# Row operands of the preceding pair re-used from a ring of four slots, and summing comparisons in the preparation of a graph-network kernel

## The chip, the cores and the metric

One core of a Trainium2 chip runs the whole program. The metric is the device time of one execution in microseconds (us); less is better. Three runs of the kernel before gave a median of 1769.53 us (1767.42 to 1770.1).

## The reference, cut to what matters

Four graph-network blocks follow one another on 3125 nodes of 256 features. Each normalises the rows, applies a ReLU, runs its layer and adds the result to `x`:

```
h = relu(layernorm(x)); x = x + sage2(h, src, dst)                # two mean-aggregating layers
h = relu(layernorm(x)); x = x + gcn(h, edge_weight, src, dst)     # sum of weighted source rows
h = relu(layernorm(x)); x = x + inter(h, edge_attr_64, src, dst)  # messages, layer norm, a small MLP
h = relu(layernorm(x)); x = x + maxk(h, src, dst)                 # top 32 of 256, mean of source rows
```

All four sum rows of source nodes into destination nodes over the same 50000 edges (`src`, `dst`, the latter sorted; `edge_weight` for the second). The kernel therefore builds two dense matrices of 3200 x 3200 first: the count of edges from a source to a destination (f16, exact) and the sum of their weights (f32). The aggregations are then matrix products with them. The change lies in this build and in the preparation of its tables.

## The kernel before, in words

**Preparation (from line 872 on VectorE, 1311 on PE).** The 50000 edges lie in 391 tiles of 128 edges. For each edge VectorE computes a row key and a column key from destination and source, and splits the weight into three bf16 parts that sum to it. PE transposes them (L1324), so that `col[:, a, t]` holds, with one edge per partition, the keys (C_S, C_Q) and weight parts (C_W0 to C_W2) of tile t. Column 0 of `col` is zero: a tile that matches nothing. Since the edges are sorted by destination, eight consecutive destinations (half a pair) lie in a run of tiles. VectorE counts, for the limits of each of the 200 pairs (128 to a column of the table, two columns, `nb`), how many tiles lie under the limit: a comparison that writes a row of 391 zeros and ones (L935) and a reduction that sums it (L936). From these counts it makes a packed word per pair (first tile x 512 + end tile) in small one-column instructions (L944 to L955), each waiting for the one before by a semaphore (`Chain`). PE turns the words into one row (L1341), VectorE casts them to integers (L957), and the engines load them into registers at the start of each chunk (`pairs_of`).

**Build (the loops `long_loop(.., NT)`, 25 chunks of `PER` = 8 pairs).** A pair n covers 16 destinations, 8 in each of two halves. For a tile of edges VectorE writes three one-hot operands (`hot`, L967): a row matrix S of 128 edges x 128 (L969), S times the first weight part (L970), and a column matrix Q of 128 edges x 400 or 200 (L972; 200 columns for the first half alone). ACT and GpSimd multiply S by the second and third weight parts: GpSimd the third part of the first set (L611) and both of the second set (L615, L616), ACT the rest (L655, L660, L662). PE then issues four products per tile (L1348): S against Q into the counts' bank, and the three weighted copies against Q into the weights' bank. A pair has a first set U0 (its first tile, 200 columns), one or more rest sets, and a second set U1 (400 columns); U0 and U1 are "fixed", the rest sets are a loop whose bounds come from the packed word. The operand buffers are doubled by the pair's parity (`par`). Within a pair a second rest set goes into the same buffer as the first: VectorE waits (L984) until PE has used it.

The order on each engine is written out by hand: PE runs U0, rest, U1 of pair n (`build_pair`, L1351); VectorE runs U0, rest, then waits for PE to have used U1 of pair n - 2 (L988) and writes U1 (`hot_pair`, L975); GpSimd copies the pair's weights to `w_col` (L607), drains, and multiplies (`weigh_pair`, L604); ACT weighs pair n and then takes the finished banks of pair n - 1 to SBUF (`take`, L644). Between pairs PE does the rows of the first layer: a transpose after the fifth pair of a chunk (L1386), a small product after the eighth (L1392, L1394); GpSimd does a subtraction for it after the seventh (L601). SP stores each chunk's blocks to HBM (L448, L450), pads edge features there (L433), and loads the first two transposed blocks at the end (L457).

**After the build** five passes of aggregation (L1440, L1434) and dense layers follow; they are untouched.

## Time and profile before

| | |
|---|---|
| median of 3 runs | 1769.53 us |
| the profiled execution | 1772.75 us |
| its span, first to last instruction | 1770.9 us |
| PE busy, 11007 matmuls | 1634.4 us (92%) |
| VectorE (DVE) busy | 1067.5 us (60%) |
| ScalarE (ACT) busy | 696.6 us (39%) |
| GpSimd (POOL) busy | 363.3 us (21%) |
| DMA | 245.55 MB, 139 GB/s mean |

The profile lists instructions of one execution: line of the kernel, engine, operation, `out<-in` by tile name, shapes, count, busy time, mean duration of one, idle time of the engine before them and what ended it. PE is TensorE's matmul, PEld its weight load, which overlaps it. The ends of matmuls are modelled, since they are pipelined. Register, branch and semaphore instructions are not counted as busy. In a timeline a row is a run of like instructions: start, duration, engine, line, count, and in brackets the idle time before it. `e_buf` is the tile that holds the ring of one-hot operands, `ps` is PSUM, `front` holds `col`.

### The profile page before, as it was taken

What the parts mean: (1) busy time and instruction counts of PE and PEld (TensorE: products, weight loads), DVE (VectorE), ACT (ScalarE), POOL (GpSimd) and SP (SyncE); (2) the same over time, 40 slices, a digit from 0 to 9 for tenths busy, and PEclk for the clock granted to TensorE, in tenths of its full rate; (3) what the DMA queues carried; (4) which work ended last, traced back from release to release, by engine and by line L of the source; (5) the groups of instructions that cost most, each with busy time, mean ns of one, the idle gap of its engine ahead of it and who ended that gap; (6) DMA issues with size and microseconds to landing.
All of it is one profiled execution on the core that took longest, in us unless ns stands there. A gap on an engine that the chain in (4) does not pass through costs nothing.

```text
span 1770.9 us, 43586 instructions
## 1 busy us (share of the span) xinstructions
PE 1634.4 (92%) x11007; PEld 1213.6 (69%) x11008; DVE 1067.5 (60%) x3434; ACT 696.6 (39%) x1918; POOL 363.3 (21%) x925
## 2 busy tenths in 40 slices
PE   2899899898898999999999999999989999987996
PEld 1444445454445777768887888888878888864885
DVE  6888999898896122233334666666626777774111
ACT  5777788787784111111111222222224444440000
POOL 0555567565562000000000000000002111110000
PEclk8899999999999999999998999999999999997998
DMA  4256565565658766643334665565522222211444
GB/s 128 68 135 159 131 166 149 135 171 131 170 135 222 221 201 185 186 148 119 121 130 140 177 181 153 165 182 163 153 79 78 77 77 77 77 57 45 154 152 147
DMA packets 353540, 245.55 MB, mean 139 GB/s; under 512 B 195242, under 2 KB 337382, under 8 KB 353510
## 3 DMA queue, kind: packets, MB, share of 16 engines
q1 hardware_dynamic: 353510, 245.19, 48.3%
q8 instruction: 14, 0.23, 0.1%
q14 instruction: 16, 0.13, 0.0%
HBM read 138.17 MB, written 99.31 MB: 134 GB/s over the span
## 4 chain that ended last, share of the span: by engine, by line
issue 64%; PE 18%; DVE 7%; POOL 4%; DVEq 3%; POOLq 2%; ACT 0%; ACTq 0%
PE ps L1348 8%; PE ps L1440 8%; DVE e_buf L969 2%; POOL work L630 2%; DVE e_buf L972 2%; DVE e_buf L970 2%; POOLq L608 1%; POOL e_buf L611 1%; PE ps L1394 1%; DVEq L969 1%; DVEq L972 1%; PE ps L1392 1%; DVEq L983 1%; POOL e_buf L616 0%; DVEq L970 0%
## 5 line engine op out<-in xcount | busy, mean ns | idle before, releaser
L1440 PE MATMUL ps<-arena 128*128 128x256 f16 (+1 forms) x5000 | 605.2, 274 | 13.3 <-DVE arena L1288 7.0
L1440 PEld LDWEIGHTS ps<-arena 128*128 128x128 f16 x5000 | 488.0, 98 | 110.9 <-issue 42.7
L1348 PE MATMUL ps<-e_buf 128*128 128x400 bf16 (+1 forms) x2476 | 424.1, 309 | 46.6 <-DVE e_buf L972 23.8
L1348 PEld LDWEIGHTS ps<-e_buf 128*128 128x128 bf16 x2476 | 205.9, 98 | 253.6 <-DVE e_buf L972 68.3
L1434 PE MATMUL ps<-arena 128*128 128x256 f32 x1250 | 280.9, 382 | 0.6 <-ACT arena L783 0.6
L1434 PEld LDWEIGHTS ps<-arena 128*128 128x128 f32 x1250 | 237.4, 192 | 33.1 <-ACT arena L783 1.3
L630 POOL TENSOR_TENSOR work<-work 128x256 f32<-128x256 f32 x75 | 54.9, 732 | 989.6 <-ACT work L828 989.6
L972 DVE TENSOR_SCALAR e_buf<-iota,off_g,front 128x400 bf16<-128x400 f16 (+1 forms) x619 | 232.5, 376 | 0.0
L970 DVE TENSOR_SCALAR e_buf<-iota,front 128x128 bf16<-128x128 f16 x619 | 205.2, 332 | 0.0
L969 DVE TENSOR_SCALAR e_buf<-iota,front 128x128 bf16<-128x128 f16 x619 | 174.8, 282 | 41.9 <-PE ps L1348 36.2
L615 POOL TENSOR_SCALAR e_buf<-e_buf,w_col 128x128 bf16<-128x128 bf16 x200 | 96.7, 484 | 122.0 <-DVE e_buf L969 121.0
L660 ACT ACTIVATE e_buf<-e_buf,front 128x128 bf16<-128x128 bf16 x219 | 88.2, 403 | 76.6 <-DVE e_buf L969 73.8
L611 POOL TENSOR_SCALAR e_buf<-e_buf,w_col 128x128 bf16<-128x128 bf16 x200 | 88.2, 441 | 70.0 <-issue 68.9
L646 ACT ACTIVATE work<-ps 128x400 f16<-128x400 f32 x200 | 97.7, 489 | 12.3 <-PE ps L1348 12.2
L1113 DVE TENSOR_SCALAR rdeg<-ps 128x1 f32 (+1 forms) x25 | 4.0, 158 | 162.9 <-PE ps L1440 162.9
L647 ACT ACTIVATE arena<-ps 128x400 f32<-128x400 f32 x200 | 99.3, 496 | 0.0
L739 ACT ACTIVATE work<-ps 128x256 f32<-128x256 f32 x75 | 28.7, 383 | 178.2 <-PE ps L1414 178.2
L655 ACT ACTIVATE e_buf<-e_buf,front 128x128 bf16<-128x128 bf16 x200 | 80.9, 404 | 21.6 <-DVE e_buf L969 14.9
L734 ACT ACTIVATE small<-small 128x1 f32<-128x1 f32 x50 | 14.7, 294 | 186.1 <-DVE small L1001 186.1
L662 ACT ACTIVATE e_buf<-e_buf,front 128x128 bf16<-128x128 bf16 x219 | 85.2, 389 | 0.0
L1591 PE MATMUL ps<-work,front 128*128 128x128 f32 x600 | 80.7, 278 | 3.3 <-POOL work L630 3.2
L1304 DVE SCALAR_TENSOR_TENSOR work<-ps,rdeg,arena 128x256 f32<-128x256 f32 x25 | 12.1, 484 | 112.7 <-PE ps L1440 112.7
(206 smaller groups left out, 1772.2 us busy)
## 6 DMA issues: line engine op xcount, KB each, us to landing
arena<-turned_blocks SPq DMA_DIRECT2D x75, 800.0 KB, 4.3
wgt_blocks<-arena SPq DMA_DIRECT2D x25, 1600.0 KB, 10.3
arena<-wgt_blocks SPq DMA_DIRECT2D x25, 1600.0 KB, 8.3
cnt_blocks<-work SPq DMA_DIRECT2D x25, 800.0 KB, 5.5
turned_blocks<-arena SPq DMA_DIRECT2D x25, 800.0 KB, 3.5
e_raw<-edge_features_padded SPq DMA_DIRECT2D x25, 576.0 KB, 7.9
edge_features_padded<-in_edge_attr SPq DMA_DIRECT2D x24, 512.0 KB, 9.8
out<-arena SPq DMA_DIRECT2D x24, 128.0 KB
```

The costliest lines, as they stand in the source:

```text
L611: pool.tensor_scalar(sets_of(par, U0, 3), sets_of(par, U0, 0), w[:, 1, 0:1], 1.0, ALU.mult, ALU.mult).then_inc(s_hotP, 1)
L615: pool.tensor_scalar(sets_of(par, U1, 2), sets_of(par, U1, 0), w[:, 0, 1:2], 1.0, ALU.mult, ALU.mult)
L630: pool.tensor_tensor(GT[l + 1], GT[l], YT, ALU.add).then_inc(s_g, 1)
L646: act.activation(stage_c[par][:, t, :], cnt_ps[t % 2][:, 0:GW], ACT.Copy)
L647: act.activation(stage_w[par][:, t, :], wgt_ps[t % 2][:, 0:GW], ACT.Copy).then_inc(s_taken, 1)
L660: act.activation(sets_of(par, REST, 2), sets_of(par, REST, 0), ACT.Copy, scale=one(col[:, C_W1, :], t))
L969: dve.tensor_scalar(sets_of(par, u, 0), iota1[:, 0:P], key, None, ALU.is_equal).then_inc(s_S, 1)
L970: dve.tensor_scalar(sets_of(par, u, 1), iota1[:, 0:P], key, one(col[:, C_W0, :], t), ALU.is_equal, ALU.mult)
L972: dve.tensor_scalar(q_of(par, u), iota1[:, 0:Q_WIDE[u]], one(off_g, n), one(col[:, C_Q, :], t), ALU.add, ALU.is_equal).then_inc(s_Q, 1)
L1348: return pe.matmul(bank[:, 0:wide], sets_of(par, u, part), q_of(par, u), start=start, stop=True, skip_group_check=True)
L1434: m = pe.matmul(agg[par][:, 0:D], BLK32[par][:, b * P:(b + 1) * P], ZFULL[0][:, b * D:(b + 1) * D], start=(b == 0), stop=(b == NT - 1), sk ...
L1440: m = pe.matmul(agg[par][:, 0:wide], BLK16[par][:, b * P:(b + 1) * P], ZH[zin(i)][:, b * ZW + part * D:b * ZW + part * D + wide], start=(b ...
```

## The change

A pair's first tile is mostly the last tile of the pair before it, since the pairs follow one another in the sorted edges. Its row operand S and the three weighted copies depend on the tile alone, not on the pair; only Q does. The change keeps the rest sets' row operands in a ring of four slots (`rest_set(i, part)`, slot i mod 4) and lets the next pair's first four products read the slot of pair i - 1, with a new column matrix `q_first`. For the last rest set to be the last tile of its pair, the tables change: if the pair's first tile is the preceding pair's last one (`shared`), `u_first` is that tile, else the empty tile 0; the tile after it is the fixed set `u_next` (or tile 0); all later ones are rest sets, at least one per pair. There are now two packed words per pair: (rest, end) and (u_first, u_next). VectorE loads both, PE and ACT the first, GpSimd the second.

Per pair VectorE writes `q_first`, then waits for `s_used` 2n + 2 and writes the row matrix of `u_next`; then the rest sets as before; then the columns of `u_next`. GpSimd makes all three weighted copies of `u_next`. ACT weighs the rest sets only. PE waits for GpSimd once a pair.

In the preparation the comparison sums what it writes (`accum_out`), so that the six pairs of comparison and reduction become eight comparisons; the small instructions work on two columns at once.

```diff
@@ buffers
-RING_AT = (0, SETS + HW, 2 * SETS + HW + GW)
-RINGW = 3 * SETS + HW + 2 * GW
+SLOTS = 4
+REST_AT = 2 * SETS
+Q_AT = REST_AT + SLOTS * SETS
+RINGW = (Q_AT + 2 * HW + 4 * GW + 1) // 2
...
+        def rest_set(i, part):
+            at = REST_AT + i % SLOTS * SETS + part * P
+            return ring[:, at:at + P]
...
+            lo, many = (0, PER) if which == "rest" else (PER, PER) if which == "fixed" else (0, 2 * PER)
+            at = c * (2 * PER) + lo
...
@@ GpSimd, weigh_pair
-                pool.tensor_copy(w, col[:, C_W1:C_W2 + 1, bass.ds(first_of(pool, v), 2)])
+                pool.tensor_copy(w, col[:, C_W0:C_W2 + 1, bass.ds(low_of(pool, v), 1)].rearrange("p a o -> p (a o)"))
                 pool.drain()
-                wait(pool, s_hotS, n * 2 + 1)
+                wait(pool, s_hotS, n + 1)
                 pool.sem_inc(s_made, 1)
-                pool.tensor_scalar(sets_of(par, U0, 3), sets_of(par, U0, 0), w[:, 1, 0:1], 1.0,
-                                   ALU.mult, ALU.mult).then_inc(s_hotP, 1)
-                wait(pool, s_hotS, n * 2 + 2)
-                pool.sem_inc(s_made, 1)
-                pool.tensor_scalar(sets_of(par, U1, 2), sets_of(par, U1, 0), w[:, 0, 1:2], 1.0, ALU.mult, ALU.mult)
-                pool.tensor_scalar(sets_of(par, U1, 3), sets_of(par, U1, 0), w[:, 1, 1:2], 1.0,
-                                   ALU.mult, ALU.mult).then_inc(s_hotP, 1)
+                for k in range(3):
+                    m = pool.tensor_scalar(next_set(par, k + 1), next_set(par, 0), w[:, k:k + 1], 1.0,
+                                           ALU.mult, ALU.mult)
+                m.then_inc(s_hotP, 1)
@@ ACT, weigh_pair
-                s = first_of(act, v)
-                wait(act, s_hotS, n * 2 + 1)
-                act.activation(sets_of(par, U0, 2), sets_of(par, U0, 0), ACT.Copy, scale=one(col[:, C_W1, :], s)
-                               ).then_inc(s_hotA, 1)
-                with act.Fori(s + 2, end_of(act, v)) as t:
+                with act.Fori(high_of(act, v), end_of(act, v)) as t:
@@ VectorE, tables
             def tiles_under(into, row, n, op):
-                chain(dve.tensor_scalar(count_scratch, ps[:, row, 0:ET], nidx[:, n:n + 1], None, op))
-                chain(dve.tensor_reduce(into, count_scratch, AX.X, ALU.add))
+                chain(dve.tensor_scalar(count_scratch, ps[:, row, 0:ET], nidx[:, n:n + 1], 0.0, op, ALU.add,
+                                        accum_out=into))
...
+            chain(dve.scalar_tensor_tensor(out=f, in0=first, scalar=1.0, in1=last, op0=ALU.add, op1=ALU.min))
+            chain(dve.tensor_tensor(shared, prev, f, ALU.is_equal))
+            chain(dve.tensor_tensor(more, last, f, ALU.is_gt))
+            chain(dve.tensor_tensor(split, half, f, ALU.is_ge))
+            chain(dve.tensor_tensor(shared, shared, more, ALU.mult))
+            chain(dve.tensor_tensor(shared, shared, split, ALU.mult))
+            chain(dve.tensor_tensor(u_first, f, shared, ALU.mult))
+            chain(dve.tensor_tensor(g, f, shared, ALU.add))
...
+            for k in range(2):
+                chain(dve.tensor_copy(both[:, :, k, :], ps[0:1, 2, k * 2 * P:(k + 1) * 2 * P].rearrange(
+                    "o (c i) -> o c i", i=PER)))
+            chain(dve.tensor_copy(tab[0:1, 4 * P:6 * P], ps[0:1, 3, 0:2 * P]))
@@ VectorE, a pair
-                wait(dve, s_used, n * 2 + 1)
-                hot(n, par, U0, s, s_hotS, s_hotQ)
+                wait(dve, s_used, n * 2 + 1)
+                edge_cols(n, q_first(par), HW, high_of(dve, fixed_), s_hotQ)
+                u = low_of(dve, fixed_)
+                wait(dve, s_used, n * 2 + 2)
+                edge_rows(next_set(par, 0), u, s_hotS)
 
                 dve.reg_add(room, k_reg, 1)
-                with dve.Fori(s + 2, end_of(dve, v)) as t:
+                with dve.Fori(high_of(dve, v), end_of(dve, v)) as t:
                     wait(dve, s_restused, dve.snap(room, min_val=1, max_val=1 << 20))
-                    hot(n, par, REST, t, s_restS, s_restQ)
+                    edge_rows(rest_set(i, 0), t, s_restS)
+                    dve.tensor_scalar(rest_set(i, 1), iota1[:, 0:P], one(col[:, C_S, :], t), one(col[:, C_W0, :], t),
+                                      ALU.is_equal, ALU.mult)
+                    edge_cols(n, q_rest(par), GW, t, s_restQ)
...
-                wait(dve, s_used, n * 2 + 2)
-                hot(n, par, U1, s + 1, s_hotS, s_hotQ)
+                edge_cols(n, q_next(par), GW, u, s_hotQ)
@@ PE, tables: six one-column products in place of four
@@ PE, build_pair
-                product(counts, HW, par, U0, 0, start=True)
-                product(weights, HW, par, U0, 1, start=True)
-                wait(pe, s_hotA, n + 1)
-                product(weights, HW, par, U0, 2)
-                wait(pe, s_hotP, n * 2 + 1)
-                product(weights, HW, par, U0, 3).then_inc(s_used, 1)
+                product(counts, HW, rest_set(i - 1, 0), q_first(par), start=True)
+                product(weights, HW, rest_set(i - 1, 1), q_first(par), start=True)
+                product(weights, HW, rest_set(i - 1, 2), q_first(par))
+                product(weights, HW, rest_set(i - 1, 3), q_first(par)).then_inc(s_used, 1)
...
                 wait(pe, s_hotQ, n * 2 + 2)
-                product(counts, GW, par, U1, 0)
-                product(weights, GW, par, U1, 1)
-                wait(pe, s_hotP, n * 2 + 2)
-                product(weights, GW, par, U1, 2)
-                product(weights, GW, par, U1, 3).then_inc(s_used, 1)
+                product(counts, GW, next_set(par, 0), q_next(par))
+                wait(pe, s_hotP, n + 1)
+                product(weights, GW, next_set(par, 1), q_next(par))
+                product(weights, GW, next_set(par, 2), q_next(par))
+                product(weights, GW, next_set(par, 3), q_next(par)).then_inc(s_used, 1)
```

GpSimd also clears the ring's last slot once at the start, which the first pair's products read.

## Rows read from the trace of the kernel before

**Rows 1.** The build stage: busy us (instructions) per engine, clock, DMA share, GB/s.

```profile
47.50:553.70 506.20, 462.06 (x2671) 235.48 (x2672) 465.53 (x1859) 405.29 (x1136) 304.06 (x825) 0.99 0.56 146
```

**Rows 2.** The same view of one plain chunk of the build.

```profile
118.30:136.10 17.80, 16.79 (x99) 8.87 (x98) 17.80 (x73) 14.81 (x41) 12.23 (x33) 1.00 0.64 166
```

**Rows 3.** Groups of the build: count, busy us, mean ns, idle before.

```profile
L1348 PEld LDWEIGHTS ps<-e_buf 128*128 128x128 bf16 x2476 | 205.9, 98 | 253.6 <-DVE e_buf L972 68.3 <-POOL e_buf L611 44.6 <-POOL e_buf L616 24.0
...
L969 DVE TENSOR_SCALAR e_buf<-iota,front 128x128 bf16<-128x128 f16 x619 | 174.8, 282 | 41.9 <-PE ps L1348 36.2 <-issue 4.5
```

**Rows 4.** Waits of the build: who for whom, us, times, longest.

```profile
PEld ps L1348 <- POOL e_buf L611: 44.6, 101, 1.0
DVE e_buf L969 <- PE ps L1348: 36.2, 19, 2.9
```

**Rows 5.** Timeline of VectorE over one plain pair (start, us, engine, line).

```profile
300.05 0.31 DVE L969 TENSOR_SCALAR e_buf<-iota,front 128x128 bf16<-128x128 f16 x1
...
300.24 0.30 DVE L970 TENSOR_SCALAR e_buf<-iota,front 128x128 bf16<-128x128 f16 x1
...
300.46 0.35 DVE L972 TENSOR_SCALAR e_buf<-iota,off_g,front 128x200 bf16<-128x200 f16 x1
...
302.20 0.31 DVE L969 TENSOR_SCALAR e_buf<-iota,front 128x128 bf16<-128x128 f16 x1
```

**Rows 6.** Timeline of GpSimd: two pairs, and one cycle without waits.

```profile
301.98 0.49 POOL L615 TENSOR_SCALAR e_buf<-e_buf,w_col 128x128 bf16<-128x128 bf16 x1 [0.25 <-DVE e_buf L969]
302.44 0.46 POOL L616 TENSOR_SCALAR e_buf<-e_buf,w_col 128x128 bf16<-128x128 bf16 x1
302.85 0.19 POOL L607 COPY w_col<-front 128x4 f32 x1
303.39 0.49 POOL L611 TENSOR_SCALAR e_buf<-e_buf,w_col 128x128 bf16<-128x128 bf16 x1 [0.35 <-issue]
...
305.03 0.66 POOL L601 TENSOR_TENSOR arena<-arena 128x256 f32 x1
305.64 0.18 POOL L607 COPY w_col<-front 128x4 f32 x1
...
307.82 0.19 POOL L607 COPY w_col<-front 128x4 f32 x1 [0.38 <-issue]
...
309.56 0.18 POOL L607 COPY w_col<-front 128x4 f32 x1
```

**Rows 7.** Timeline, PE's weight loads around a chunk's border.

```profile
131.34 0.29 PEld L1392 LDWEIGHTS ps<-b_early,ones_row 1*128 1x128 f32 x2 [0.33 <-issue]
...
132.72 3.37 PEld L1348 LDWEIGHTS ps<-e_buf 128*128 128x128 bf16 x24
```

**Rows 8.** Timeline of PE, the transpose of each chunk, three chunks running.

```profile
208.49 0.38 PE L1386 MATMUL ps<-ident,arena 128*128 128x128 f32 x2
...
226.32 0.38 PE L1386 MATMUL ps<-ident,arena 128*128 128x128 f32 x2
...
247.58 0.38 PE L1386 MATMUL ps<-ident,arena 128*128 128x128 f32 x2
```

**Rows 9.** Timeline, PE's weight loads in a pair with two rest sets.

```profile
183.02 0.45 PEld L1348 LDWEIGHTS ps<-e_buf 128*128 128x128 bf16 x4 [0.16 <-DVE e_buf L972]
...
184.86 0.11 PEld L1348 LDWEIGHTS ps<-e_buf 128*128 128x128 bf16 x2 [1.39 <-DVE e_buf L972]
...
185.77 0.11 PEld L1348 LDWEIGHTS ps<-e_buf 128*128 128x128 bf16 x2 [0.46 <-DVE e_buf L972]
...
186.27 0.11 PEld L1348 LDWEIGHTS ps<-e_buf 128*128 128x128 bf16 x2 [0.39 <-POOL e_buf L616]
```

**Rows 10.** Groups of VectorE in the tables of the preparation.

```profile
L935 DVE TENSOR_SCALAR work<-ps,nidx 128x391 f32<-128x391 f32 x6 | 3.8, 625 | 3.3 <-PE ps L1336 3.1
L936 DVE TENSOR_REDUCE tab_f<-work 128x1 f32<-128x391 f32 x6 | 3.4, 559 | 0.2
...
L945 DVE TENSOR_TENSOR tab_f<-tab_f 128x1 f32<-128x1 f32 x2 | 0.3, 159 | 0.1
```

More of the change, by code:

```diff
@@ L934, in tiles_under @@
             def tiles_under(into, row, n, op):
-                chain(dve.tensor_scalar(count_scratch, ps[:, row, 0:ET], nidx[:, n:n + 1], None, op))
-                chain(dve.tensor_reduce(into, count_scratch, AX.X, ALU.add))
+                chain(dve.tensor_scalar(count_scratch, ps[:, row, 0:ET], nidx[:, n:n + 1], 0.0, op, ALU.add,
+                                        accum_out=into))
+            (first, half, last, prev, f, more, split, shared, g, inside, u_first, u_next, rest, end, pair, fixed,
+             e_first, e_end, edges) = (tab_f[:, k, :] for k in range(19))
@@ L938, in _ @@
             for nb in range(2):
-                first, half, end, early, start, until, pair, edges = (
-                    tab_f[:, 8 * nb + k:8 * nb + k + 1] for k in range(8))
-                tiles_under(first, 0, 2 * nb, ALU.is_lt)
-                tiles_under(half, 0, 2 * nb + 1, ALU.is_lt)
-                tiles_under(end, 1, 2 * nb + 1, ALU.is_le)
-                chain(dve.tensor_scalar(first, first, float(ET - 1), None, ALU.min))
-                chain(dve.tensor_tensor(early, half, first, ALU.is_le))
@@ L946, in _ @@
-                chain(dve.scalar_tensor_tensor(out=end, in0=first, scalar=1.0, in1=end, op0=ALU.add, op1=ALU.max))
-                chain(dve.scalar_tensor_tensor(out=start, in0=first, scalar=1.0, in1=early, op0=ALU.add,
-                                               op1=ALU.subtract))
-                chain(dve.tensor_scalar(until, end, 1.0, None, ALU.add))
-                chain(dve.scalar_tensor_tensor(out=until, in0=start, scalar=3.0, in1=until, op0=ALU.add, op1=ALU.max))
-                chain(dve.scalar_tensor_tensor(out=pair, in0=start, scalar=512.0, in1=until, op0=ALU.mult,
-                                               op1=ALU.add))
@@ L954, in _ @@
-                chain(dve.scalar_tensor_tensor(out=edges, in0=first, scalar=512.0, in1=end, op0=ALU.mult,
-                                               op1=ALU.add))
-            dve.wait_ge(s_prep_pe, PE_TABLES + 2)
-            chain(dve.tensor_copy(tab[0:1, :], ps[0:1, 2, 0:4 * P]))
-            assert chain.v == PREP_STEPS
+                o = slice(nb, nb + 1)
+                tiles_under(first[:, o], 0, 2 * nb, ALU.is_lt)
+                tiles_under(half[:, o], 0, 2 * nb + 1, ALU.is_lt)
@@ new lines, in _ @@
+            chain(dve.tensor_tensor(shared, shared, split, ALU.mult))
+            chain(dve.tensor_tensor(u_first, f, shared, ALU.mult))
+            chain(dve.tensor_tensor(g, f, shared, ALU.add))
+            chain(dve.tensor_tensor(inside, g, last, ALU.is_lt))
+            chain(dve.tensor_tensor(u_next, g, inside, ALU.mult))
+            chain(dve.scalar_tensor_tensor(out=rest, in0=g, scalar=1.0, in1=last, op0=ALU.add, op1=ALU.min))
+            chain(dve.tensor_scalar(end, last, 1.0, None, ALU.add))
@@ new lines, in _ @@
+            chain(dve.scalar_tensor_tensor(out=pair, in0=rest, scalar=512.0, in1=end, op0=ALU.mult, op1=ALU.add))
+            chain(dve.scalar_tensor_tensor(out=fixed, in0=u_first, scalar=512.0, in1=u_next, op0=ALU.mult,
+                                           op1=ALU.add))
+            chain(dve.tensor_scalar(e_first, first, float(ET - 1), None, ALU.min))
+            chain(dve.scalar_tensor_tensor(out=e_end, in0=e_first, scalar=1.0, in1=last, op0=ALU.add, op1=ALU.max))
+            chain(dve.scalar_tensor_tensor(out=edges, in0=e_first, scalar=512.0, in1=e_end, op0=ALU.mult,
+                                           op1=ALU.add))
@@ L1324, in transpose_rows_of @@
                     pe.transpose(ps[:, a % 4, c * P:(c + 1) * P], from_[:, c, :], ident[:, :]).then_inc(s_prep_pe, 1)
[L1326 removed]
+            for a, from_ in enumerate((part_f[:, 1], part_f[:, 8], part_f[:, 7], rows[:, 2])):
                 transpose_rows_of(a, from_)
@@ L1346, in _, with product @@
             start_walk(pe, mybir.EngineType.PE)
-            def product(bank, wide, par, u, part, start=False):
-                return pe.matmul(bank[:, 0:wide], sets_of(par, u, part), q_of(par, u), start=start, stop=True,
-                                 skip_group_check=True)
+            def product(bank, wide, rows_, cols, start=False):
+                return pe.matmul(bank[:, 0:wide], rows_, cols, start=start, stop=True, skip_group_check=True)
             def build_pair(c, i, v):
```

99 lines of the change are left out of this document (52 added, 47 removed).

## The prediction

> **What bounds the kernel now.** Times by stage come first. The build of the adjacency blocks (200 pairs of 8-node groups, 25 chunks of eight pairs) takes 506.2 us of the 1770.9 us span at a granted clock of 0.99, TensorE's upper level of 2.4 GHz [rows 1]. Only this stage and the end of the preparation before it are edited, so everything is decided there. The same row seems to show two full engines: VectorE busy for 465.5 us and PE for 462.1 us. A window on one chunk without disturbance tells them apart: VectorE is busy for 17.80 of 17.80 us [rows 2]. PE's busy time is modelled. What it can do is read where its operands lay ready: 24 weight loads of the build, two whole pairs of twelve products, take 3.37 us, 1.69 us a pair [rows 7], while a pair of the same kind takes VectorE 2.15 us from one first instruction to the next [rows 5]. So VectorE sets the pace, and PE could go about a fifth faster.
>
> Next, the pace over many pairs. PE's transposes L1386 come once a chunk: 17.83 us apart in a plain chunk, 21.26 us in one that holds a pair with two rest sets [rows 8]. The count of L969 (619 = 2 x 200 + 219) says that 19 pairs have a second rest set [rows 3], and VectorE waits for PE before a row matrix 19 times, 36.2 us in all [rows 4]. The stage is thus 25 x 17.8 = 445 us plus 61 us; with some 3 us for its start, each of the 19 costs about 3.1 us.
>
> **The change, part by part.** Its effect per pair first; By the new table formulas the reference's own destinations give 219 rest sets before and after, and a shared tile in 186 of 200 pairs. PE issues the same 2476 products [rows 3].
>
> *VectorE per pair.* Gone: the first set's row matrix and its weighted copy, and the weighted copy of the second fixed set. Start to start these take 0.19, 0.22 and 0.22 us [rows 5] (the third by the row of its shape): 2.15 - 0.63 = 1.52 us remain. The new wait and the second table word add register work that no row prices: at least 0; at most one more instruction slot, 0.22 us, so 1.5 to 1.75. I take 1.55, as most register work runs ahead. Eight pairs and 0.45 us at a chunk's border (17.65 of the 17.8 are 8 x 2.15 plus this): 12.9 us a chunk. The load of 16 instead of 8 table words falls there and lies in that slack.
>
> *GpSimd per pair.* Three products before and after, now in a row behind one matrix. The cycle without a wait is 1.74 us, copy to copy [rows 6]. With VectorE busy beside it: 0.54 from copy to first product, 0.46 from product to product twice, 0.41 from the last to the next copy, 1.87 us [rows 6]. Add per chunk the subtraction L601 (0.61 to the next copy) and some 0.4 at the border: 8 x 1.74 + 1.0 = 14.9, or 8 x 1.87 + 1.0 = 16.0 us. I take the middle, 15.5, since VectorE will be idle part of the time.
>
> The Trainium skill (GPSIMD Engine Reference, Key points) says that GpSimd shares its SBUF interfaces with VectorE and contends with VectorE instructions that run in a two-port mode. By that rule alone the chunk would be the 16.0 us; the two cycles of [rows 6] agree with its direction, and the sum above does without it.
>
> *PE per chunk.* 8 x 1.69 = 13.5, the transposes 0.4, the own-row products with the gap before them 0.33 + 1.38 = 1.7 (131.34 to 132.72) [rows 7]: 15.6 us. ACT loses one of its weighted copies per pair, and its 15 us of chunk fall further.
>
> *The chunk.* PE at 15.6 and GpSimd at 15.5 stand level, each with bumps at another pair. Today one engine leads and the chunk is 0.15 us over its work; with two level I allow 0.7: 16.3 us. Bounds: 15.6 (perfect overlap) and 17.2 (GpSimd at 16.0, and 1.2 us of waits between the two). Gain 1.5 us on 24 chunks (the first, filling, counted as nothing): **-36 us** (-53 to -14).
>
> *The pair with two rest sets.* VectorE may not write the second set before PE used the first, before and after. PE ends the first set's products near 183.7 us (four loads from 183.02), starts the second's at 184.86, and would be through at 185.7: 2.0 us that stay. Then it waits 0.46 us for the last set's columns at 185.77, and 0.39 us for its weighted copies at 186.27 [rows 9]. That row matrix is now written and weighted ahead of the rest sets, and the next pair's first products need only one new column matrix. So 3.1 becomes 2.0 us: **18 x 1.1 = -20 us** (0.5 to 1.5 each: -9 to -27; one of the 19 lies in the first chunk).
>
> *Waits that move.* The wait for the pair before last (s_used, 2n + 2) moves from the end of a pair to its second instruction. Behind it in VectorE's queue stand the row matrix, all rest sets and the last columns. From the release: row matrix 0.2, three GpSimd products 1.4, two semaphore hops 0.3, so the weighted copies are there after 1.9 us. PE gets to them after one pair (1.69), the next pair's first products (0.34), its rest (0.68) and one product: 2.9 us. The wait is covered by 1.0 us; with L601 in between, by 0.4.
>
> *Preparation*, on the path of everything. Gone: 12 count instructions, 6 x (0.66 + 0.60) us, and 16 small ones at 0.195 [rows 10] (0.04 us between instructions included): 10.7 us. New: 8 counts at 0.66 and 17 small: 8.6. Two more one-column PE products and three copies of 256 elements in place of one of 512: +1.0, an estimate by L935's 0.62 us for 391 elements. A summing comparison has no row on VectorE: it costs nothing more, or at most the reduction that it replaces, 0.56 each, 4.5 us. I take 0.06 each, as it writes one column: **-0.5 us** (-1.1 to +3.4).
>
> The Trainium skill (VectorE: DVE Perf Modes, Two Vector instructions with no wait between them) counts an operation that writes out its accumulator as two instructions. By that each count would cost one small instruction more, 0.2 us, and the part would end at +0.5 us. No row here shows it.
>
> *After the build* nothing is edited. SP's queue must, between the last two chunks, load two transposed blocks, keep them and store the last chunk; that is hidden in the last chunk and in the first block's products, at no cost. If that cover is gone, it is late by no more than the 1.5 us by which the chunk gets shorter.
>
> Sum: -36 - 20 - 0.5 = -56.5 us. The profiled execution took 1772.75 us (span 1770.9), 3.2 us over the median of 1769.53; taken off the median: **1713 us**.
>
> **The rivals.** *A. VectorE or GpSimd keeps the pace.* Register work or contention holds a pair at 1.9 us or more: a chunk of 17.0 us, gain 24 x 0.8 + 18 x 1.0 + 0.5 = 38 us: 1732 us. For it: register work is not counted as busy, so no row shows how much of VectorE's 2.15 us it sets, and 1.87 us is the GpSimd cycle seen beside a busy VectorE. Against it: where PE had fallen behind, GpSimd itself ran at 1.74 us. Chance 0.2.
>
> *B. PE's full pace.* Chunks of 15.7 us and 1.5 us per double rest: -50 - 27 - 1 = -78, 1691 us. For it: 1.69 us was sustained over two pairs. Against: GpSimd's 1.74 us plus its border work. Chance 0.12.
>
> *C. Slower: GpSimd's three products.* The place is PE's wait for s_hotP before the second product of the last set; now all three copies hang on it, the first set's no longer comes early. If products beside VectorE's builds stretched to 0.65 us, a cycle would be 0.54 + 2 x 0.65 + 0.6 = 2.44 us, 0.29 us over today: 200 x 0.29 - 20 = +38, 1807 us. It decides from a cycle of 2.25 us, which takes products of 0.59. For it: L601 of the same engine takes 0.66 us [rows 6]; against it: no product spacing there is over 0.46. Chance 0.04.
>
> *D. The change doesn't do what it says.* If tiles were seldom shared, rest sets would multiply and eat the gain, near 1770 us. The count of 186 of 200 speaks against it. The reading of PE's busy time as real work (462 of 506) would leave at most 44 us, near A. Chance of D 0.02.
>
> **How the numbers follow.** The forecast gets 0.62; its own range is 1697 to 1727. The range 1691 to 1738 also takes in A, and B's centre; C, D and the far half of B are left out. About 0.2% (3.5 us) is what a measurement of this kernel can tell from no change: faster 0.94, same 0.02, slower 0.04.
>
> **What would show it.** L969 falls from 619 to 419 with L970's counterpart at 219; the build's window shrinks from 506 to about 450 us; VectorE's share in a plain chunk falls from 100% to about 80%, and its wait for PE rises from 19 times to once in most pairs; L1386's successors stand about 16.3 us apart in plain chunks and 2 us more in those with a double rest; the weight loads of a plain pair run through in 1.7 to 1.9 us, and PE's wait for GpSimd's first copy (44.6 us [rows 4]) is gone. Wrong would be: chunks still at 17.5 us or more; GpSimd cycles over 2.2 us with PE waiting for its last product in every pair; preparation longer than before.

## The result and the profile after

The changed kernel takes **1709.24 us** (median of 4 runs, 1707.5 to 1710.39), the kernel before 1769.82 us on the same chip: a ratio of 0.9652, 95% interval 0.9633 to 0.9670. The forecast was 1713 us. The profiled execution took 1709.9 us, its span is 1708.1 us. So the sum came out, but two of its parts were wrong in opposite directions: the build by 17 us, what follows it by 11. From the first product of a stage to the first of the next, in the two traces (the build to the end of its last product; the 2.2 us from there to the next stage are the same in both):

| us | before | after | difference | forecast |
|---|---|---|---|---|
| to the first product of the build | 48.27 | 47.67 | -0.6 | -0.5 |
| build | 505.4 | 432.3 | **-73.1** | -56 |
| first stage after it: its first five blocks | 50.1 | 53.1 | +3.0 | 0 |
| blocks 6 to 24 | 161.6 | 161.6 | 0 | 0 |
| from block 25 to the next stage | 18.8 | 24.2 | **+5.3** | 0 |
| the other four stages | 984.5 | 987.0 | +2.5 | 0 |

The stage windows of the kernel after, the build and the stage behind it (us; busy us of PE, PEld, DVE, ACT, POOL with their counts; clock, DMA share, GB/s), and one plain chunk in the same view, to be read against [rows 1, 2]:

```profile
47.70:480.00 432.30, 412.68 (x2671) 247.20 (x2671) 358.58 (x1258) 333.76 (x935) 266.72 (x824) 0.99 0.65 167
482.20:721.00 238.80, 221.70 (x1556) 170.22 (x1556) 50.42 (x166) 30.91 (x75) 0.00 (x0) 0.96 0.68 194
...
248.38:264.01 15.63, 15.63 (x106) 9.82 (x104) 13.65 (x50) 12.85 (x37) 10.75 (x34) 1.00 0.74 183
```

VectorE does 1258 instructions in place of 1859. In the plain chunk it is busy 13.65 of 15.63 us, where it was busy 17.80 of 17.80. PE's row shows 15.63 of 15.63 as well, but the ends of its products are modelled; the runs below tell the two apart. Its groups and GpSimd's in the build, with the counts that the prediction asked for (419 and 219 for the 619 of [rows 3]); PE's wait for GpSimd's first copy [rows 4] is gone from the waits:

```profile
L997 DVE TENSOR_SCALAR e_buf<-iota,off_g,front 128x400 bf16<-128x400 f16 (+1 forms) x618 | 222.0, 406 | 33.2 <-PE ps L1377 30.6 <-issue 2.6
L628 POOL TENSOR_SCALAR e_buf<-e_buf,w_col 128x128 bf16<-128x128 bf16 x600 | 220.9, 382 | 162.5 <-DVE e_buf L993 156.1 <-issue 6.3
...
L993 DVE TENSOR_SCALAR e_buf<-iota,front 128x128 bf16<-128x128 f16 x419 | 111.4, 273 | 40.5 <-PE ps L1377 26.8 <-issue 6.8
...
L1013 DVE TENSOR_SCALAR e_buf<-iota,front 128x128 bf16<-128x128 f16 x219 | 75.1, 343 | 0.0
```

The pace, by PE's transposes of each chunk as in [rows 8]: three plain chunks of 15.63 us, one with two double rests (19.67), one with one (17.73).

```profile
217.12 0.38 PE L1412 MATMUL ps<-ident,arena 128*128 128x128 f32 x2
232.75 0.38 PE L1412 MATMUL ps<-ident,arena 128*128 128x128 f32 x2
248.38 0.38 PE L1412 MATMUL ps<-ident,arena 128*128 128x128 f32 x2
264.01 0.38 PE L1412 MATMUL ps<-ident,arena 128*128 128x128 f32 x2
283.68 0.38 PE L1412 MATMUL ps<-ident,arena 128*128 128x128 f32 x2
301.41 0.38 PE L1412 MATMUL ps<-ident,arena 128*128 128x128 f32 x2
```

VectorE's timeline at the border of a plain chunk (start, us, idle before it in brackets), and its queue's load of the table words, for the kernel after and then, in the last fence, for the kernel before:

```profile
250.90 0.84 DVE L993 TENSOR_SCALAR e_buf<-iota,front 128x128 bf16<-128x128 f16 x2
251.66 0.30 DVE L1013 TENSOR_SCALAR e_buf<-iota,front 128x128 bf16<-128x128 f16 x1
251.88 0.73 DVE L997 TENSOR_SCALAR e_buf<-iota,off_g,front 128x400 bf16<-128x400 f16 x2
253.99 0.33 DVE L997 TENSOR_SCALAR e_buf<-iota,off_g,front 128x200 bf16<-128x200 f16 x1 [1.39 <-PE ps L1377]
```

```profile
L391 DVEq TENSOR_LOAD <-tab x25: 1100/1105/1371, 45.5 to 460.9; - x25
```

```profile
L379 DVEq TENSOR_LOAD <-tab x25: 598/602/869, 46.3 to 529.4; - x25
```

The border's 1.39 us is the only long pause of VectorE in a plain chunk, and 1.1 us of it is the load of 16 words (it runs from 252.56 us; 8 words took 0.6). The page puts the pause down to PE, which had long been done. The other two pauses of the chunk are 0.15 us each, and between them instruction follows instruction. So VectorE's queue, with its loads and register work, fills the chunk although the busy share is only 87%: without 1.2 us for the load and its gaps, (15.63 - 1.2) / 8 = 1.80 us a pair.

### The profile page after: what moved, and what is told of

It is laid out like the page before. It is cut to its first block, busy times and chain, and to the rows that moved or that the text cites. A ratio compares the mean times of both kernels' runs of the same rounds, so it can differ in the third digit from the quotient of the medians.

```text
span 1708.1 us, 41810 instructions
## 1 busy us (share of the span) xinstructions
PE 1587.9 (93%) x11011; PEld 1227.7 (72%) x11012; DVE 960.3 (56%) x2841; ACT 625.3 (37%) x1718; POOL 326.2 (19%) x926
## 3 DMA queue, kind: packets, MB, share of 16 engines
q1 hardware_dynamic: 353510, 245.19, 50.1%
## 4 chain that ended last, share of the span: by engine, by line
issue 60%; PE 33%; DVE 3%; POOL 2%; DVEq 1%; SPq 0%; POOLq 0%; DMA 0%; ACT 0%
PE ps L1377 21%; PE ps L1466 8%; POOL work L643 2%; PE ps L1420 1%; PE ps L1418 1%; DVE e_buf L997 0%; DVE work L943 0%; PE ps L1412 0%; PE ps L1639 0%; SPq L419 0%; PE ps L1353 0%; DVE small L1253 0%; PE ps L1365 0%; DVE e_buf L1013 0%; PE ps L1370 0%
## 5 line engine op out<-in xcount | busy, mean ns | idle before, releaser
L1377 PE MATMUL ps<-e_buf 128*128 128x400 bf16 (+1 forms) x2476 | 374.8, 308 | 23.6 <-DVE e_buf L997 23.5
L1377 PEld LDWEIGHTS ps<-e_buf 128*128 128x128 bf16 x2476 | 217.6, 98 | 169.6 <-DVE e_buf L997 51.6
L628 POOL TENSOR_SCALAR e_buf<-e_buf,w_col 128x128 bf16<-128x128 bf16 x600 | 220.9, 382 | 162.5 <-DVE e_buf L993 156.1
L997 DVE TENSOR_SCALAR e_buf<-iota,off_g,front 128x400 bf16<-128x400 f16 (+1 forms) x619 | 222.3, 405 | 35.0 <-PE ps L1377 30.6
L993 DVE TENSOR_SCALAR e_buf<-iota,front 128x128 bf16<-128x128 f16 x419 | 111.4, 273 | 40.5 <-PE ps L1377 26.8
L669 ACT ACTIVATE e_buf<-e_buf,front 128x128 bf16<-128x128 bf16 x219 | 88.3, 403 | 106.8 <-DVE e_buf L993 106.4
L670 ACT ACTIVATE e_buf<-e_buf,front 128x128 bf16<-128x128 bf16 x219 | 85.3, 390 | 0.0
L1617 PEld LDWEIGHTS ps<-work,front 128*128 128x128 f32 x600 | 74.9, 196 | 7.0 <-POOL work L643 4.7
L1013 DVE TENSOR_SCALAR e_buf<-iota,front 128x128 bf16<-128x128 f16 x219 | 75.1, 343 | 0.0
L836 ACT ACTIVATE work<-ps,mlp_col 128x128 f32<-128x128 f32 x150 | 46.8, 364 | 58.0 <-PE ps L1617 58.0
```

Of the source, the lines that this page charges most:

```text
L628: m = pool.tensor_scalar(next_set(par, k + 1), next_set(par, 0), w[:, k:k + 1], 1.0, ALU.mult, ALU.mult)
L669: act.activation(rest_set(i, 2), rest_set(i, 0), ACT.Copy, scale=one(col[:, C_W1, :], t))
L670: act.activation(rest_set(i, 3), rest_set(i, 0), ACT.Copy, scale=one(col[:, C_W2, :], t)).then_inc(s_restA, 1)
L993: return dve.tensor_scalar(into, iota1[:, 0:P], one(col[:, C_S, :], t), None, ALU.is_equal).then_inc(s_S, 1)
L997: dve.tensor_scalar(into, iota1[:, 0:wide], one(off_g, n), one(col[:, C_Q, :], t), ALU.add, ALU.is_equal).then_inc(s_Q, 1)
L1377: return pe.matmul(bank[:, 0:wide], rows_, cols, start=start, stop=True, skip_group_check=True)
```

## Experiments: who sets the pace of the build

Ratios are to the kernel before; the changed kernel has 0.9652, and 0.001 is 1.77 us. "Against after" is the difference of the two ratios.

**The sums alone**, in the kernel before:

```
-chain(dve.tensor_scalar(count_scratch, ..., nidx[:, n:n + 1], None, op))
-chain(dve.tensor_reduce(into, count_scratch, AX.X, ALU.add))
+chain(dve.tensor_scalar(count_scratch, ..., nidx[:, n:n + 1], 0.0, op, ALU.add, accum_out=into))
```

> The kernel before with the summing comparisons alone: the six reductions of its tables are gone, everything else stands. If the sum costs the comparison nothing, the tables are 6 x 0.60 = 3.6 us shorter and the time falls by as much (about 1766 against 1769.8 us); if each sum costs a small instruction, 6 x 0.4 = 2.4 us are left. Rival: the sum costs as much as the reduction it replaces: no difference, within 1 us.

Measured: 0.9988 (0.9979 to 0.9997). The build starts at 44.29 us for 48.27: -4.0 us, six reductions of 0.56 us with their gaps. Only 2.1 us of it show in the time; in the trace a later stage, the fourth pass, is 2.4 us longer (the end of the next section has this stage in all traces).

**The ring alone**: the same lines the other way round in the changed kernel.

> The changed kernel with comparison and reduction as two instructions again: eight reductions more, 8 x 0.60 = 4.8 us on the path of everything: about 1714 us against 1709 us. Rival (the sum is as dear as the reduction): the same time as the changed kernel, 1709 us. Either way the ring carries over nine tenths of the gain.

Measured: 0.9690 (0.9676 to 0.9703). The build starts at 52.72 us, 5.05 later, 0.63 for each of eight reductions, and lasts 432.1 us as with the sums. So the two parts of the change don't touch each other: all of the build's gain is the ring's. VectorE's groups in the preparation of the changed kernel show what a sum costs:

```profile
L943 DVE TENSOR_SCALAR_CACHE_REDUCE work<-ps,nidx 128x391 f32<-128x391 f32 x8 | 5.0, 625 | 3.4 <-PE ps L1365 3.2
...
L943 DVE DVE_READ_ACCUMULATOR work<-ps,nidx 128x1 f32 x8 | 0.7, 83 | 0.0
```

The comparison takes the 625 ns of L935 [rows 10], and a second instruction of 83 ns reads the accumulator out. The Trainium skill (VectorE: DVE Perf Modes, Two Vector instructions with no wait between them) counts two instructions here; the trace agrees. The second starts before the first has ended, so that counts follow each other every 0.668 us, where a comparison and the start of its reduction stood 0.660 apart: it adds 0.01 us, not the 0.2 us that the prediction worked out from the rule.

**One product less on PE** (the last weight of each rest set left out):

```
-product(weights, GW, rest_set(i, 2), q_rest(par))
-product(weights, GW, rest_set(i, 3), q_rest(par)).then_inc(s_restused, 1)
+product(weights, GW, rest_set(i, 2), q_rest(par)).then_inc(s_restused, 1)
```

> The changed kernel without the third weight part's product of the rest sets (the weights lose their last eight bits or so; GpSimd, VectorE and ACT do all that they did). If PE alone paces the build, 219 products of 400 columns at 0.169 us go: 37 us less, about 1672 us. Rival, as the prediction had it (GpSimd and PE level): at most 10 us less, over 1699 us.

Measured: 0.9608 (0.9590 to 0.9625), -8 us against after. The plain chunk stays at 15.63 us; only chunks with two rest sets got shorter, by 0.2 us a set. PE alone does not hold the pace.

**One VectorE instruction more** in each pair, into a tile that nobody reads:

```
+dve.tensor_scalar(unused[:, i % 4, :], iota1[:, 0:P], one(col[:, C_S, :], u), one(col[:, C_W0, :], u),
+                  ALU.is_equal, ALU.mult)
 edge_cols(n, q_next(par), GW, u, s_hotQ)
```

> The changed kernel with one more row-matrix instruction per pair on VectorE, into a tile that nobody reads, ahead of the last columns. If PE paces the build and VectorE has the 0.4 us per pair that a plain chunk shows as idle: 0 to +5 us. Rival (VectorE's issue sets the pace): 200 x 0.22 = +44 us, about 1753 us.

Measured: 0.9733 (0.9718 to 0.9747). The plain chunk is 16.70 us: 1.07 more, 0.134 for each of eight instructions. The build is 25 us longer, the time only 14: the rest came back behind the build, 7.6 us of it in the first stage there, as the section on that shows.

**One and two GpSimd products more** in each pair, into tiles that nobody reads:

```
+for k in range(1):            # the second kernel: range(2)
+    pool.tensor_scalar(unused[:, 2 * par + k, :], next_set(par, 0), w[:, 0:1], 1.0, ALU.mult, ALU.mult)
 for k in range(3):
     m = pool.tensor_scalar(next_set(par, k + 1), ...)
```

> The changed kernel with one more product per pair on GpSimd, ahead of its three, into a tile that nobody reads. If GpSimd has real room (it waits 156 us for VectorE's row matrix in the build, 0.78 us a pair), one product of 0.38 us costs 0 to +5 us. Rival (the prediction: GpSimd level with PE, a cycle of 1.75 us): the cycle becomes 2.1 us against PE's 1.70, a chunk 8 x 2.1 + 1.0 = 17.8 us, +40 us or more, about 1750 us.

> Two more products per pair on GpSimd. If the room is 0.4 us of true waiting per pair, the second product is no longer covered: +0.35 us for some 160 plain pairs, +50 us or so over the run with one more. Rival (GpSimd level with PE from the start): both products cost in full, 2 x 0.38 x 200 = +150 us, about 1860 us.

Measured: 0.9742 (0.9727 to 0.9756) and 1.0071 (1.0052 to 1.0089); plain chunks of 16.65 and 19.15 us. The first eight extra products last 8 x 0.417 = 3.3 us and cost 1.0, so GpSimd had some 2.3 us of room in a chunk (an estimate). The next eight cost 2.5 of their 3.1 us: now GpSimd paces, and PE waits for its last product. From the waits of the kernel with two more:

```profile
PEld ps L1380 <- POOL e_buf L631: 113.2, 147, 1.4
...
PE ps L1380 <- POOL e_buf L631: 59.2, 128, 1.0
```

This is the state that the prediction's rival C describes: 19.15 / 8 = 2.39 us a pair, and the kernel is slower than before.

**VectorE one instruction less**: the rest set's weighted copy goes, PE's work stays as it is.

```
-dve.tensor_scalar(rest_set(i, 1), ..., one(col[:, C_S, :], t), one(col[:, C_W0, :], t), ALU.is_equal, ALU.mult)
...
-product(weights, GW, rest_set(i, 1), q_rest(par))
+product(weights, GW, rest_set(i, 0), q_rest(par))
```

> Left out: VectorE's weighted copy of each rest set (219 instructions) is not written, and TensorE reads the set's plain rows in its place, so the first weight's products are not the reference's; TensorE's work is as in the changed kernel. Theory (VectorE and TensorE stand level at the changed kernel's 15.63 us a plain chunk): one issue slot of 0.134 us is taken from each pair of VectorE's queue, 1.07 us a chunk, but TensorE's own work of 15.55 us then holds the chunk: 15.5 to 15.6 us, 0 to -3 us in the time. Rival (VectorE alone paces, TensorE has room): chunk 14.56 us, -27 us. Rival (GpSimd holds it): chunk unchanged, and its waits for VectorE's rows (156 us in the changed kernel) fall away.

**Both less**: that, and PE's product with the copy left out.

> Left out: VectorE's weighted copy of each rest set and TensorE's product with it (219 of each). Theory (VectorE and TensorE level, GpSimd close behind): VectorE's chunk falls by 1.07 us to 14.56 and TensorE's by 8 x 0.17 = 1.35 us to 14.2; GpSimd, whose cycle has some 0.25 us of room a pair at 15.63 us, then sets the end between 14.6 and 15.2 us: -10 to -27 us. Rival (VectorE's queue does not pace): as the kernel with one product less on TensorE alone, -8 us, plain chunk 15.63 us. If GpSimd already holds the pace: plain chunk 15.6 us as well, but with GpSimd no longer waiting for VectorE.

Measured: 0.9563 (0.9543 to 0.9583) and 0.9507 (0.9487 to 0.9527). A plain chunk of each:

```profile
228.51:243.98 15.47, 15.47 (x105) 10.22 (x104) 12.09 (x41) 13.25 (x37) 10.93 (x34) 1.00 0.75 193
```

```profile
223.31:238.16 14.85, 14.81 (x97) 8.80 (x96) 12.03 (x41) 12.86 (x38) 10.97 (x34) 1.00 0.77 200
```

With VectorE relieved, the plain chunk falls by 0.15 us only, to 15.47: pair after pair then takes PE 1.70 us, with a constant rest at the border. That is PE's own floor. With PE relieved too it falls to 14.85 us. So VectorE (15.63) and PE (15.47) stand all but level in the changed kernel, and GpSimd, whose work is unchanged in both, fits into 14.85. What holds the chunk at 14.85 no run takes apart. In time the first of them is -16 us, not the 0 to -3 that was expected: the build is 8.0 us shorter (0.15 in each plain chunk, more in those with two rest sets and in the first), and the other 8 lie behind the build.

**The table loaded twice**, to price the load at the border:

```
+again = pairs_of(dve, mybir.EngineType.DVE, c, "both")
 packed = pairs_of(dve, mybir.EngineType.DVE, c, "both")
```

> VectorE loads the 16 table words of a chunk twice (the second load 1.1 us, as the first in the trace of the changed kernel). Theory (the load stands in VectorE's queue at each border and is on the path): plain chunk 15.63 + 1.1 = 16.7 us, +24 to +28 us in the time. Rival (the prediction's: the load lies in slack at the border): chunk unchanged, within 3 us of the changed kernel.

Inconclusive. The line of its load shows the same 25 loads as the changed kernel's: words that nobody uses were not loaded.

```profile
L391 DVEq TENSOR_LOAD <-tab x25: 1101/1106/1377, 46.3 to 460.7; - x25
```

So it is the changed kernel once more: 0.9642 (0.9619 to 0.9665), plain chunk 15.63 us. That the load is on the path follows from the timeline above and from the instruction more, not from a run of its own.

**The copy on ScalarE**: all work kept, VectorE's weighted copy is made by ScalarE, on top of the kernel that stores first (next section).

```
-dve.tensor_scalar(rest_set(i, 1), ...)
+act.activation(rest_set(i, 1), rest_set(i, 0), ACT.Copy, scale=one(col[:, C_W0, :], t))
...
-product(weights, GW, rest_set(i, 1), q_rest(par))
 wait(pe, s_restA, k + 1)
+product(weights, GW, rest_set(i, 1), q_rest(par))
```

> All work kept: the kernel that stores the last chunk ahead of the keeps, and besides ScalarE writes the rest set's first weighted copy in VectorE's place (219 instructions moved). VectorE's chunk falls by 1.07 us, TensorE's stays at 15.55 us, ScalarE gains 8 x 0.4 = 3.2 us a chunk. Theory (TensorE is level with VectorE): plain chunk 15.5 to 15.7 us, build within 3 us of 433.9 us, time within 4 us of the kernel that only stores first (ratio 0.958 to 0.962). Rival (VectorE alone paces and ScalarE has room): -27 us. Rival (TensorE's rest products now wait for ScalarE): chunk 16.0 us or more, +10 us or more, and the pairs with two rest sets longer by 0.4 us each.

Measured: 0.9695 (0.9673 to 0.9718), 16.5 us worse than the kernel it is built on, plain chunk 16.32 us. The third case holds. From its window of a plain chunk and its waits in the build:

```profile
241.68:258.00 16.32, 16.04 (x106) 9.92 (x104) 12.11 (x41) 14.93 (x46) 10.94 (x34) 1.00 0.71 183
```

```profile
PEld ps L1378 <- ACT e_buf L673: 50.4, 120, 0.7
...
PE ps L1378 <- ACT e_buf L673: 12.3, 33, 0.5
```

ScalarE goes from 12.85 to 14.93 us of the chunk, and PE, which used to meet only two of its copies (8.6 us of waits for L670 in the changed kernel), now waits for three, ahead of its second product. ScalarE still has idle time in the chunk, so it is this wait that costs and not its load. The copy can't be moved to ScalarE for nothing in this order; another order was not tried.

## Experiments: what was lost behind the build

SP's queue around the end of the build, after and then before (its issues; L463 and L448 store the last chunk, L472 and L457 load transposed blocks, L480 and L465 keep them). The build's last product ends at 480.0 us after, at 553.7 before:

```profile
467.32 12.95 SPq L472 DMA_TRANSPOSE arena<-cnt_blocks  x2
480.42 2.42 SPq L480 DMA_DIRECT2D turned_blocks<-arena  x2
...
486.56 0.43 SPq L463 DMA_DIRECT2D cnt_blocks<-work  x1
...
494.21 5.58 SPq L472 DMA_TRANSPOSE arena<-cnt_blocks  x1
```

```profile
536.01 12.97 SPq L457 DMA_TRANSPOSE arena<-cnt_blocks  x2
549.13 2.43 SPq L465 DMA_DIRECT2D turned_blocks<-arena  x2
...
554.92 0.43 SPq L448 DMA_DIRECT2D cnt_blocks<-work  x1
```

The two transposing loads hold the queue 13 us in both. Before, the last chunk was long enough to hide them, and the store was issued 1.3 us behind the build's end; now it is 6.6 us late, and the first block's counts are waited for. The lateness reaches PE in two ways: PE waits 4.0 us for VectorE in the first block, and 5.3 us for the fifth block's transposed load. SP, which waits for the same store, issues that load at 520.11 us, 37.9 us into the stage; before, it was 34.9 us into it (590.73 us), and PE met no wait for it. From the waits of that stage after, and the load after and before:

```profile
DVE rdeg L1142 <- DMA cnt_blocks<-work: 9.7, 1, 9.7
PE ps L1466 <- DMA arena<-cnt_blocks: 5.3, 1, 5.3
```

```profile
520.11 3.28 SPq L472 DMA_TRANSPOSE arena<-cnt_blocks  x1
```

```profile
590.73 3.18 SPq L457 DMA_TRANSPOSE arena<-cnt_blocks  x1
```

In both kernels the sixth block starts 15.2 us behind that load. Two kernels move SP's work, each from the changed kernel:

```
 sp.wait_ge(s_prep, PREP_STEPS)
+pad_edges(NT - 1)
 for b in range(2):
     sp.wait_ge(s_store_c[b], 16 * NPAIR)
     load_turned(b, b)
+store(NT - 1, 0, pad=False)
 for b in range(2):
     keep(b, 0, b)
-store(NT - 1, 0)
```

> The changed kernel with SP's order changed at the end of the build: the last padding goes ahead of the two transposing loads, and the last chunk's stores ahead of the two stores of the transposed blocks. In the changed kernel the last count store starts 5.9 us after the last product (1.3 us before the change), and the first four blocks of the first aggregation end 3.0 us later than before. If SP's lateness makes these 3 us: about 3 us less, 1706 us. Rival (they come from elsewhere, code loading or the clock): no change, within 1.5 us.

The other one does the loads and keeps of the two transposed blocks right after chunk 1 is stored:

```
+for c in range(2):
+    store(c, c)
 for b in range(2):
-    sp.wait_ge(s_store_c[b], 16 * NPAIR)
+    sp.wait_ge(s_store_c[b], 16)
     load_turned(b, b)
...
+with sp.Fori(1, NPAIR) as j:
+    for c in range(2):
+        store(j * 2 + c, c)
 store(NT - 1, 0)
```

> The changed kernel with the two transposing loads and their stores moved from the last chunk to the second: they need only the first two chunks' counts. SP is then free when the last chunk ends. If SP's lateness counts: 3 to 8 us less, 1701 to 1706 us, since before the change too the first five blocks took 8 us more than five steady ones. Rival (the loads delay the stores of chunks 2 and 3 and so the build, or the excess is code loading): no change, or some us more.

Measured: 0.9602 (0.9589 to 0.9615) and 0.9617 (0.9604 to 0.9630). The first five blocks take 47.6 and 47.7 us, some 5.4 less than in the changed kernel and 2.4 less than in the kernel before. So SP's order at the end of the build holds these 5.4 us. That the store alone makes the 3.0 us between before and after is not shown: the kernel with two GpSimd products more, whose chunks are long again, issues it 1.0 us ahead of the stage and still takes 53.1 us, with PE waiting 5.6 us for the fifth block's load (issued 37.0 us into the stage); the one with one more takes 46.5. Nor do the 2.4 us show that the store cost anything before: VectorE met no wait for stored blocks there, and a pause of another kind, the subject of the next paragraph, stood in the fourth block. By the ratios the two are 8.9 and 6.2 us below the changed kernel, by their traces 3.6 and 6.8; executions of one kernel lie up to 5.5 us apart. The first of the two is, all but level with the second, the fastest kernel here with all its work: 1701.67 us, against 1709.24 and 1769.82 (each beside its own runs of before).

**The other 5.3 us** lie at the end of that stage. VectorE's timeline there, after:

```profile
705.61 0.16 DVE L1142 TENSOR_SCALAR rdeg<-ps 128x1 f32<-128x1 f32 x1 [6.37 <-PE ps L1466]
708.58 0.16 DVE L1143 RECIPROCAL rdeg<-rdeg 128x1 f32<-128x1 f32 x1 [2.81 <-issue]
```

and in the kernel before:

```profile
776.27 0.16 DVE L1113 TENSOR_SCALAR rdeg<-ps 128x1 f32<-128x1 f32 x1 [6.37 <-PE ps L1440]
776.50 0.16 DVE L1114 RECIPROCAL rdeg<-rdeg 128x1 f32<-128x1 f32 x1
```

Two unedited instructions that follow each other stand 2.8 us apart now, with nothing waited for. PE, which needs the result, is idle for 3.79 us in place of 1.06, and then runs slower. Its timeline and the windows around it (clock in the third column from the right), after:

```profile
709.36 0.69 PE L1527 MATMUL ps<-ident,work 128*128 128x128 f32 x2 [3.79 <-DVE work L1145]
...
713.50 3.18 PE L1449 MATMUL ps<-W_early,work 128*128 128x512 f32 x4 [0.47 <-ACT work L747]
```

```profile
697.00:705.00 8.00, 8.00 (x60) 6.20 (x59) 1.86 (x6) 1.03 (x3) 0.00 (x0) 1.00 0.34 117
705.00:713.00 8.00, 3.74 (x14) 2.19 (x11) 2.23 (x7) 0.59 (x2) 0.00 (x0) 0.76 0.31 104
713.00:721.07 8.07, 5.41 (x11) 2.16 (x11) 1.84 (x6) 1.60 (x4) 0.00 (x0) 0.82 0.00 0
```

and PE's timeline before:

```profile
777.29 0.44 PE L1501 MATMUL ps<-ident,work 128*128 128x128 f32 x2 [1.06 <-DVE work L1116]
...
780.02 1.98 PE L1423 MATMUL ps<-W_early,work 128*128 128x512 f32 x4 [0.47 <-ACT work L739]
```

The idle time gives 2.7 of the 5.3 us; the rest is products at the lower level of the clock (the mean of 0.76 to 0.82 mixes 1.2 and 2.4 GHz), the four of L1449 at 3.18 us for 1.98.

Which kernels have it? From block 25 to the next stage, over all traces: 18.8 us in before and the sums alone, whose VectorE instructions in the build are the old ones; 22.9 to 24.6 us in the changed kernel and all seven kernels with the same VectorE instructions in the build (ring alone, one product less on PE, one and two products more on GpSimd, both SP orders, the void table load); and 18.8 us again in all four kernels that changed VectorE's instructions in the pair (one more; one less; both less; the copy on ScalarE). But no trace is without such a pause. In the kernel with one more, a pause of 4.1 us before the same reciprocal stands around the fourth block (547.7 us), as in the sums alone (4.9 us) and in the kernel before, where PE is idle for 3.5 us behind it:

```profile
587.24 0.16 DVE L1114 RECIPROCAL rdeg<-rdeg  x1 [4.35 <-issue]
```

In the three with one less it stands before another instruction, 2.7 to 3.0 us into the next stage. The row below is from the kernel with VectorE one instruction less, where PE then waits 0.7 us; the other two have pauses of 3.0 and 2.7 us at the same place:

```profile
710.50 0.69 DVE L1089 TENSOR_REDUCE scale<-front 128x2 f32<-128x512 f32 x1 [2.75 <-issue]
```

So the pause goes by VectorE's program, not by data or load, and the change moved it and did not add it: what it cost in the fourth block can't be told apart from the wait for the fifth block's load that stands behind it. In the 4 us of the pause the changed kernel's DMA view has one transfer on an instruction queue, of 17 in the whole execution; the kernel before has one around its own pause:

```profile
q14 instruction: 1, 0.01, 0.8%
```

That VectorE waits there for the next piece of its code is the reading that fits; no run tested it by itself. The last 2.5 us lie in the fourth pass, 314.4 us before and 316.8 after. Over the traces it takes 313.1 to 316.9 us, and 313.2 in the kernel whose second table load was not made, which is the changed kernel once more. So they can't be put down to the change; what makes them stays open.

## Why the prediction was right, and where it was not

*The chunk: at the edge of its range, with another engine in the lead.* Forecast 16.3 us (15.6 to 17.2), measured 15.63; 24 chunks give -52.8 us for -36. That VectorE's queue sets the pace before, and that fewer instructions in it shorten the chunk, was right; that PE and GpSimd would then lead, with VectorE at 80%, was not: VectorE still leads, PE stands just behind it, and GpSimd has room. VectorE's pair was put at 1.55 us, 1.75 at most, and is 1.80. The subtraction took three start-to-start times from [rows 5]; an instruction taken out or put in is worth less, 0.134 us in the run with one more, and (2.15 - 1.80) / 3 = 0.12 here, probably since the register work stays and the instructions left next to each other are longer (the 400-wide column matrix 438 ns, before 387); which of the two it is no run tells. The load of the table words "falls at the border and lies in that slack": there is no slack, it stands in the queue for 1.1 us. Both errors would have made the chunk longer. What undid them: GpSimd was put at 15.5 us and fits into 14.85, since its products, put 0.46 us apart by [rows 6], follow each other after 0.36 in a row behind one matrix; and 0.7 us was allowed for two level engines, where the chunk lies 0.16 over PE's floor of 15.47. That these errors left the chunk inside the range is luck. The rivals split the truth: the pace is VectorE's register-laden queue, as in A, but at the chunk of B (15.7 us). PE's chunk of 15.6 us was right by 0.1.

*Two rest sets: right.* Forecast 2.0 us for 3.1; measured 37.7 us over the 18 extra sets behind the first transpose, 2.1 each, where it was 55.2 us: -17.5 us for -20. The first chunk and the end of the build, counted as nothing, gave -2.8 us more.

*The moved wait: covered, as forecast.* VectorE's wait for PE before a row matrix went from 19 times to 39 (26.8 us), not to "once in most pairs". Of that, 22.6 us (19 times) stand before a second rest set, and the moved wait itself was met once, for 0.7 us.

*Preparation: right*, -0.6 us for -0.5 (the prediction's own terms add up to -0.6): the sums give 4.0 to 5.05 us, the larger table takes it back.

*After the build: wrong.* "At no cost, late by no more than 1.5 us" is the step that failed, by 10.8 us, 2.5 of which are no effect of the change. The cover was named and its loss was not worked out: SP's chain of loads, keeps and pads lasts as long as ever, the chunk that hid it does not. The first five blocks are 3.0 us longer, and the two SP orders give them back with 2.4 us more. And an unedited place lost 5.3 us to a pause that moves with VectorE's program; the trace of before has this pause in the fourth block, but nothing in it shows where a new program will put it.

The build gained 17 us more than forecast, the rest lost 11 that were forecast as nothing: the 1713 us are closer to 1709 than their terms were, and that is luck. Rivals C and D are out: GpSimd waits for VectorE (156 us), not the other way round, and the rest sets number 219.

## What to carry to other kernels

An instruction removed from a queue of register-addressed instructions was worth about what one more costs there (0.12 and 0.134 us here), not its start-to-start time (0.21); put one in and measure. When an engine is relieved, write down the next three engines' full loads, with table loads and register work in them: here VectorE, PE, GpSimd and ScalarE stood at 15.63, 15.47, at most 14.85 and some 13 us of a chunk. And a stage that gets shorter must be checked for the queue that hid in it: issue the store that the next stage waits for at once ahead of the keeping that is waited for later. The SP order that stores first together with a VectorE program whose pause does not stand at the end of the stage was run only with the copy on ScalarE: its first stage takes 227.7 us, against 238.9 in the changed kernel and 230.5 before. Without the slower build it was not tried.

## Unexpected of the hardware

- A load of table words into VectorE's registers takes 0.6 us for 8 words and 1.1 us for 16, and stops the queue; the profile shows it as idle time and may name another engine for it.
- A pause of 2.7 to 4.9 us without a wait stands in the first stage behind the build or just behind it in all 14 traces; its place, in the fourth block, in the last or at the start of the next stage, changes with VectorE's program. At the end of the stage, behind 3.8 us of idle PE, the granted clock fell to the lower level, which doubled the pause's price.
- In 19 of the 25 chunks, a row matrix of VectorE takes 0.7 us in place of 0.25 while GpSimd's subtraction runs: the pair of L993 at 250.90 us above (0.84 us for both) stands beside this row of GpSimd's timeline. Beside GpSimd's products L993 takes 0.27 us on average:

```profile
250.89 0.63 POOL L617 TENSOR_TENSOR arena<-arena 128x256 f32 x1
```

The Trainium skill (GPSIMD Engine Reference, Key points) says that GpSimd shares its SBUF interfaces with VectorE and contends with VectorE instructions in a two-port mode or with two SBUF inputs; the trace agrees in that this operation holds the matrix up, but in which mode the matrix runs no run here shows.
